# One head tile of lag, fewer DVE operations in attention, and edge columns and projection tiles placed elsewhere in the FFN

## The reference, cut to what matters

```python
xn = _layernorm(x, axis=-1)
x = x + attn(xn, ...) + ffn(xn, ...)

# attn, per head, Dh = 64
q = (x @ wq_w.T + wq_b); k = (x @ wk_w.T + wk_b); v = (x @ wv_w.T + wv_b)
attn = softmax(where(x[:, :, 0] != 0, q k^T / sqrt(Dh), -inf))
out = (attn @ v) @ wo_w.T + wo_b

# ffn
h = bit_linear(x, w1)                  # 1024 -> 4096, int8-like activations, ternary weights
h = depthwise_conv1d(h, conv_w, conv_b)   # width 3, over the tokens
h = silu(h)
return bit_linear(h, w2)               # 4096 -> 1024
```

## Time and profile before

| | |
|---|---|
| median of 3 runs | 1260.81 us (1182.61 to 1311.77) |
| the profiled execution | 1182.18 us, its slowest core (core 1) has a span of 1180.6 us |
| spans of the 8 cores | 1174.3 to 1180.6 us, granted PE clock 0.991 to 0.993 |
| PE busy | 1091.4 us (92% of the span) |
| DVE busy | 890.5 us (75%) |
| ACT busy | 815.8 us (69%) |
| POOL busy | 242.8 us (21%) |
| head | about 0 to 91 us |
| rest of attention | about 91 to 645 us |
| FFN block 0 | about 646 to 756 us |
| FFN blocks 1 to 3 and the tail | about 756 to 1181 us |

### The profile page before, as it was taken

How to read it: one execution, slowest core, us unless ns; L and a number is a source line. 1 busy time by engine, 2 the same in 40 slices (tenths; PEclk the granted TensorE clock), 3 DMA queues, 4 the chain that set the end, 5 groups by cost and what they waited for, 6 DMA issues and landing times.

```text
span 1180.6 us, 28483 instructions; the slowest of 8 cores (1174.3 to 1180.6 us)
## 1 busy us (share of the span) xinstructions
PE 1091.4 (92%) x9138; PEld 593.5 (50%) x9138; DVE 890.5 (75%) x1487; ACT 815.8 (69%) x1110; POOL 242.8 (21%) x263
## 2 busy tenths in 40 slices
PE   2679999999999999999988999989999999999998
PEld 2355655655565665655555444444444444444443
DVE  5437888988887888888851788877777777878866
ACT  3578888888888899899998545456666666556300
POOL 4220000000000000000012123233333333332684
PEclk9799999999999999999999999999999999999999
DMA  8535557555463767757673344574354545453452
GB/s 220 184 53 140 168 163 197 161 151 172 165 194 89 183 152 180 189 162 203 186 170 88 117 148 154 172 233 128 114 161 134 173 136 170 136 157 88 136 185 89
DMA packets 84061, 183.06 MB, mean 155 GB/s; under 512 B 24816, under 2 KB 28944, under 8 KB 83920
## 3 DMA queue, kind: packets, MB, share of 16 engines
q1 hardware_dynamic: 79248, 172.52, 48.3%
q0 software_dynamic: 4240, 8.69, 5.0%
q10 hardware_dynamic: 432, 0.04, 0.0%
HBM read 164.44 MB, written 25.17 MB: 161 GB/s over the span
## 4 chain that ended last, share of the span: by engine, by line
PE 67%; ACT 15%; issue 7%; DVE 7%; POOL 1%; DMA 1%; ACTq 0%; DVEq 0%; POOLq 0%; SPq 0%
PE psC L914 16%; PE psA L932 15%; ACT probs L405 14%; PE psS L500 11%; PE psV L517 5%; PE psQ L449 5%; PE psA L900 4%; PE psQ L465 3%; PE psQ L458 3%; PE psC L932 2%; DVE wsum L644 1%; DMA xhead<-x 1%; DVE u_sb L1067 1%; DMA strm<-x 1%; DVE xarea L1135 1%
## 5 line engine op out<-in xcount | busy, mean ns | idle before, releaser
L405 ACT ACTIVATE probs<-psS 128x1024 bf16<-128x1024 f32 x512 | 506.6, 1023 | 69.1 <-PE psS L500 52.7
L500 PE MATMUL psS<-qz,kroll 128*128 128x512 bf16 x1024 | 304.3, 378 | 18.7 <-ACT probs L405 14.0
L914 PE MATMUL psC<-xqT,w1q_sb 128*128 128x512 bf16 x1024 | 242.4, 381 | 0.0
L517 PEld LDWEIGHTS psV<-v_sb,probs 128*128 128x128 bf16 x4096 | 183.8, 97 | 77.9 <-issue 5.0
L932 PE MATMUL psA<-w2q_sb,hq 128*128 128x512 fp8e4 x896 | 212.6, 379 | 6.4 <-DVE hq L1118 6.2
L825 POOL TENSOR_TENSOR h_act<-h_act,shb_sb 128x512 f32<-128x512 f32 x128 | 165.4, 1296 | 229.0 <-DVE hq L1118 198.1
L517 PE MATMUL psV<-v_sb,probs 128*128 128x65 bf16 x4096 | 200.4, 194 | 1.7 <-DVE cn L633 0.6
L914 PEld LDWEIGHTS psC<-xqT,w1q_sb 128*128 128x128 fp8e4 x1024 | 99.1, 98 | 115.9 <-issue 1.9
L932 PEld LDWEIGHTS psA<-w2q_sb,hq 128*128 128x128 bf16 x896 | 87.0, 98 | 113.7 <-issue 10.8
L1067 DVE SCALAR_TENSOR_TENSOR u_sb<-psC,cws,u_sb 128x511 f32<-128x511 f32 x128 | 95.7, 748 | 62.0 <-ACT u_sb L850 61.9
L850 ACT ACTIVATE u_sb<-psC,cws 128x510 f32<-128x510 f32 (+2 forms) x128 | 87.5, 684 | 53.5 <-PE psX L924 52.3
(11 more groups left out here) (109 smaller groups left out, 1057.8 us busy)
## 6 DMA issues: line engine op xcount, KB each, us to landing
strm<-w_t SPq DMA_DIRECT2D x128, 512.0 KB, 4.7
w2q_sb<-w2q_stage SPq DMA_DIRECT2D x112, 256.0 KB, 2.6
w1q_sb<-w1q_stage SPq DMA_DIRECT2D x64, 256.0 KB, 3.1
xhead<-x SPq DMA_DIRECT2D x16, 512.0 KB, 7.1
strm<-x SPq DMA_DIRECT2D x16, 512.0 KB, 4.4
xarea<-x SPq DMA_DIRECT2D x16, 512.0 KB, 5.8
res_stage<-xarea SPq DMA_DIRECT2D x16, 512.0 KB, 3.1
xarea<-res_stage SPq DMA_DIRECT2D x16, 512.0 KB, 5.8
```

What stands on the lines that cost most here:

```text
L405: s.activation(out=probs[:, (i % NP) * 1024:(i % NP + 1) * 1024], in_=psS[:, b * 1024:(b + 1) * 1024], func=AF.Exp, scale=0.125, bias=-B0) ...
L500: mm = t.matmul(psS[:, b * 1024 + hh * 512:b * 1024 + (hh + 1) * 512], kTv[:, hp % 2, kc * 128:(kc + 1) * 128], qz[:, (it % 4) * 1024 + hh ...
L517: mm = t.matmul(psV[:, hh * 512 + qt * 65:hh * 512 + (qt + 1) * 65], probs[:, o:o + 128], v_v[:, kc, 2 * hp + hh, :], start=(kc == 0 and q ...
L914: mm = t.matmul(mbank(g), w1q_sb[:, o + cc * 256:o + cc * 256 + 128], xqTv[:, cc, tb * 512:tb * 512 + 512], start=(cc == 0), stop=(cc == N ...
```

## The change

It has two parts that touch different stages.

In attention:
- The scores, `exps` and `pv` of the head come one tile later (HS = 10), the first "q" job comes after tile 5 instead of 4, and DVE's evacuations stand two tiles further behind its `stats` (i - 7 instead of i - 5).
- The two operations that fill qz become one `scalar_tensor_tensor` over 128x1024 that adds the bias and multiplies by a mask `hmask` of ones and zeros. POOL writes that mask (four small memsets) instead of clearing qz.
- The column of V that holds the key mask is written for all 16 heads with the first "v" job of a tile, and no more with the others (48 small operations fewer).
- The two reciprocals after each block become one (32 fewer); of the four small operations of an "x" task two are left.
- The planner's costs are set lower to match (`part_us`, `evac_us`, `norm_us`).

In the FFN:
- In block 0 ACT's centre tap leaves out the last column and a second activation of one column, which adds the edge term as its bias, writes it; ACT waits for f_e before it. DVE's L1079 and its semaphore f_o3 fall away.
- Projection tiles 12 to 15 come ahead of slices 1 to 4 of block 1 instead of 0 to 3, on the PE and on DVE.

```diff
-    HS = NT - 5
+    HS = NT - 6
...
-        if i == 4:
+        if i == 5:
             head_after[i].append(("q", 0, 0))
...
-    part_us = {"w": [1.2], "x": [0.9, 1.2, 0.9, 1.8], "m": [0.3], "gap": [5.0],
+    part_us = {"w": [1.2], "x": [0.9, 1.2, 0.5, 1.8], "m": [0.3], "gap": [5.0],
                "z": [0.8, 0.8, 0.9]}
-    evac_us = {"k": 0.75, "q": 1.55, "v": 0.6, "t": 0.75, "x": 0.65, "m": 1.0}
-    norm_us = 1.5
+    evac_us = {"k": 0.75, "q": 1.2, "v": 0.5, "t": 0.75, "x": 0.65, "m": 1.0}
+    norm_us = 1.3
...
-        g.memset(qz[:], 0.0).then_inc(sem("qz0"), 1)
+        for h in range(2):
+            for m in range(2):
+                g.memset(hmask[64 * m:64 * m + 64, h:h + 1],
+                         1.0 if h == m else 0.0).then_inc(sem("hmask"), 1)
+        g.wait_ge(sem("hmask"), 4)
...
-            if i >= 6:
-                exps(i - 6)
+            if i >= 7:
+                exps(i - 7)
...
             elif g == HS:
                 t.wait_ge(sem("ln_e"), 2 * NT)
+                t.wait_ge(sem("p_e"), HS)
...
-            if i >= 7:
-                pv(i - 7)
+            if i >= 8:
+                pv(i - 8)
...
-            if i >= 5:
-                scores(i - 5)
+            if i >= 6:
+                scores(i - 6)
...
-                v.tensor_scalar(qz[0:64, o:o + 512], ps[0:64, :], bqc[0:64, hp:hp + 1], None,
-                                OP.add)
-                v.tensor_scalar(qz[64:128, o + 512:o + 1024], ps[64:128, :],
-                                bqc[64:128, hp:hp + 1], None, OP.add).then_inc(sem("pq_ev"), 1)
+                v.scalar_tensor_tensor(
+                    qz[:, o:o + 1024].rearrange("p (h t) -> p h t", h=2),
+                    ps.unsqueeze(1).to_broadcast([128, 2, 512]), bqc[:, hp:hp + 1],
+                    hmask[:].unsqueeze(2).to_broadcast([128, 2, 512]),
+                    OP.add, OP.mult).then_inc(sem("pq_ev"), 1)
...
-        for i in range(NT + 6):
+        for i in range(NT + 8):
             if i < NT:
                 stats(i)
-            if i == 5:
+            if i == 7:
                 v.wait_ge(sem("cstq"), 16 * 2)
-            if 5 <= i:
-                for job in head_after[i - 5]:
+            if 7 <= i:
+                for job in head_after[i - 7]:
                     evac(job)
...
-            s.activation(out=u_sb[:, o + lo:o + hi], in_=ps[:, lo:hi],
-                         func=AF.Identity, scale=c1, bias=0.0).then_inc(sem("f_c1"), 1)
+            mid = s.activation(out=u_sb[:, o + lo:o + hi], in_=ps[:, lo:hi],
+                               func=AF.Identity, scale=c1, bias=0.0)
+            if tb == 0:
+                s.wait_ge(sem("f_e"), jc + 1)
+                e = jc * 6 + 1
+                s.activation(out=u_sb[:, o + 511:o + 512], in_=ps[:, 511:512], func=AF.Identity,
+                             scale=c1, bias=edge[:, e:e + 1]).then_inc(sem("f_c1"), 1)
+            else:
+                mid.then_inc(sem("f_c1"), 1)
...
-                if tb == 1 and NPT + jc < NT:
-                    proj(NPT + jc)
+                if tb == 1 and 1 <= jc <= NT - NPT:
+                    proj(NPT + jc - 1)
...
-                tap3.then_inc(sem("f_o3"), 1)
-                v.wait_ge(sem("f_o3"), g + 1)
-                v.wait_ge(sem("f_e"), jc + 1)
-                v.tensor_tensor(ua[:, 511:512], ua[:, 511:512],
-                                edge[:, jc * 6 + 1:jc * 6 + 2], OP.add).then_inc(sem("f_cv"), 1)
...
+        def edges(jc):
+            v.wait_ge(sem("f_m1"), jc + 1)
+            v.tensor_tensor(edge[:, jc * 6:jc * 6 + 6], psX[:, jc * 6:jc * 6 + 6],
+                            cwe[:, jc * 6:jc * 6 + 6], OP.mult).then_inc(sem("f_e"), 1)
...
             for jc in (m1_after[ti - 1] if ti >= 1 else range(2)):
+                edges(jc)
                 conv(0, jc)
```

52 lines of the change are left out of this document (22 added, 30 removed).

## The result

The changed kernel takes 1162.01 us in the median of four runs. Its ratio to the kernel before, taken over comparable runs, is 0.9828, with a 95% interval of 0.9814 to 0.9842: 1.7% faster, some 20 us. (Slow runs are left out of every ratio: 1306.88 us of after, in which the four cores of one die had a granted clock of 0.833 to 0.839 and the others 0.995 to 0.997, and 1260.81 and 1311.77 us of before, which account for its high median.) The profiled execution took 1159.86 us, where the forecast was 1159 and the one of before took 1182.18. By the ratio the forecast is 2 to 3 us too low. Direction and size are near it, but as a sum of terms that missed on both sides: over the cores they add up to 21 us, where 23 were forecast. Times "over the cores" are means over the eight cores of the profiled execution.

The account below looks back on a forecast made before the run. It took a ring of PE, DVE, POOL and ACT to bound the head, mostly the PE the rest: 1182.2 - 14.1 (head) - 3.3 (rest of attention) - 2.0 (block 0) - 3.6 (step to block 1) = 1159.2, given as 1159; range 1151 to 1169.

Parts of the forecast that it names:

- Steps 1 to 4: Head: the predicted chain through first exponential at 42.9, norm(8) at 43.8 and head's end at 76.1, 15.1 us earlier.
- The -14.1: Head: the forecast's term for its total change in us, including the cost of one step fewer done there.
- step 5: Head: one step fewer is done by its end (HS = 10), costing 0.98 to 1.14 us, taken as 1.0.
- A: Rival in the head: it gains less, with a term of -7.8 us; chance 0.17.
- step 4: Head: norm(8) to the first exponential behind it falls from 38.6 to 32.3 us, including 3.3 from shorter waits.
- of 6.0 us and some smaller ones I take 3.3: Rest of attention: of the PE's waits for DVE's evacuations, lighter DVE work saves 3.3 us; bounds 0 and 7.
- Rival C: Attention and step to block 1: DVE's relief counts in full (-7), no late w2q (-5.3), total 1154; chance 0.20.
- rival D: Attention: the qz operation's double PSUM read through a broadcast makes DVE the bound, slower than before; chance 0.02.
- The 0.9 taken off for POOL: Block 0: gain cut by 0.9 of 2.9 us because `amax` may now wait for POOL, leaving -2.0.
- B: Rival in block 0: the round trip between DVE and ACT bounds it, +3 to +5 us; chance 0.13.
- delay x tiles 14 and 15 by some 3 us on SP and POOL, which costs DVE about 1 us where it waits anyway: Step to block 1: moved evacuations make these x tiles late, but the roughly 1 us falls in DVE's existing waiting.
- the 3.6 us over the cores: Step to block 1: second product begins at 784.7 instead of 788.33, a gain of 3.6 us; bounds -5.3 and 0.

## Why the prediction was right or wrong

**The sum.** That 1159 lies so near to 1159.86 is in part luck. The head gave 1.7 us less than forecast and the step to block 1 2.5 less, the rest of attention 1.5 and block 0 0.9 more, and 1159.86 is the lowest of the four runs of the changed kernel. Two steps of the prediction failed: what the PE's waits for DVE are worth in the rest of attention, with no term for the planner's new costs, and the wait of DVE at the step to block 1 that was held to cost nothing.

**The head: right in mechanism and places, a little large.** Steps 1 to 4 forecast the first exponential at 42.9 (43.27), norm(8) at 43.8 (44.19), waits of 1.05 around the "k" jobs (1.04 twice), the end at 76.1 (76.29), and the run with the order alone shows that this is the cause. The -14.1 was too large for two reasons. The profiled core of before ends its head at 91.2, 1.0 us later than the mean over the cores, and the slowest core of the whole execution need not be the one with the slowest head. And the exponential done later (step 5) cost 1.4 us, the difference of 13.8 at the head's end and 12.4 at the 37th exponential, not 1.0. The rival with a head of -7.8 (A, chance 0.17) is out: the end of the head came 13.8 us earlier over the cores.

The 3.3 us in step 4 are two waits, 2.98 and 2.46, less twice 1.05. That they were long because of the slow "k" was my estimate. The traces show the clock beside it: on the profiled core of before the first three "k" jobs of the head take 3.62, 3.60 and 3.04 us at granted clocks of 0.50 (34.80 to 38.42), 0.50 (55.77 to 59.30) and 0.61 (74.00 to 77.00), and the fourth 1.89 at 1.00 (87.83 to 89.70). On that of the changed kernel only the first is at 0.50, the next three take 1.67 to 1.89 at 1.00, and both waits are 1.04. What sets the granted clock, no run shows.

**The rest of attention: sign right, the term mis-sized and its cause incomplete.** The step that failed is "of 6.0 us and some smaller ones I take 3.3". The waits that name DVE were only a part; the same jobs' weight loads stood 20.6 us in front of psQ, under "issue". The relief by itself gives 5.0 where 3.3 was put. The forecast took the planner's new costs as following the operations and gave them no term: they cost 4.8 us, half of the 9.6 that relief and new order give together. The gain of the new order behind the head had no term either (3.5 alone). So the measured 4.8 is 9.6 less 4.8, and that it lies near 3.3 is no sign that the term was understood. Rival C had "all waits of the PE for it" at 7, where those that name DVE alone came to 10.8, and with the loads the waits fell by 17.7 for the 9.6 us.

**The qz operation**: 1.28 us against 1.25, 32 times, so rival D is out. The line against it, that every PSUM source takes 1.5 ns per element or less, did not fit, where 256 elements take 0.48 us (1.9 ns); it was right for operations of 512 (0.75 us, 1.5 ns) and 1024 (1.28 us).

**Block 0: right, on the safe side.** 2.9 against 2.0. By hand the PE waited 3.6 us for edges, it waits 2.4. The 0.9 taken off for POOL is borne out: on the profiled core `amax` took 1.52 to 2.17 us in five slices, each time ending 1.1 us behind POOL's addition, where on that of before it had 1.22 throughout, and taking the additions out gives 1.1. Without POOL the block is thus 4.0 us shorter than before, where the count by hand had 2.9: that part was too small, and POOL's was right. The rival in which the round trip between DVE and ACT bounds the block, at +3 to +5 us (B, chance 0.13), fell: the round trip is there as forecast, 0.6 us in 31 slices, but the PE waits only 2.4 us for edges, so it has the longer way.

**The step to block 1: wrong.** The step that failed is "delay x tiles 14 and 15 by some 3 us on SP and POOL, which costs DVE about 1 us where it waits anyway". DVE does not wait anyway there: between the last fold and the scales its work is on the path, and on each of the eight cores the addition for tile 14 meets one of its operations. The additions for tiles 14 and 15 moved from well ahead of the fold (they ended at 773.52 on the profiled core, the fold began at 775.85) onto `amax`, fold or evacuation, and took 2.31 us or more ahead of the evacuation, 1.95 on the fold or 1.0 on `amax`. Of the 3.6 us over the cores 1.1 was left. The sign "no wait at `chain_rows`" failed with it (1.55 us on the profiled core), that of 1 to 2 us for w2q held (1.98). The arrangement that I had in mind exists: with POOL out of the way the step is 29.3 us on every core, 2.7 less than before, and the remaining 0.9 to my 3.6 is partly the first rounded pair, for which the PE waits 1.56 to 1.76 us once w2q is early. The forecast counted on POOL's addition stretching an operation of DVE in block 0 alone (the 0.9 us taken off); the fold has two SBUF inputs like `amax`, and on cores 3 and 7 it takes 2.64 us instead of 0.69 beside the addition. The 16 matmuls behind the rows took 5.04 us before at a granted clock of 0.71 (783.45 to 788.33); in the changed kernel the clock there is 1.00 (760.30 to 765.40), and the 15 that were recorded take 3.40.

## What to carry to other kernels

After moving work later on one engine, follow the whole ring of its buffer (evacuation, store, load, the helper engine's operation) to where it now lands in time, and look what stands there on the engine whose operations get longer beside the helper's, as DVE's fold did here (2.64 us instead of 0.69 beside POOL's addition): 2.4 us of POOL off the path before became 2 us on it. Price a scheduler's new costs as an edit of their own, with the old costs as the first experiment; in these runs the costs nearer to the durations made the slower plan. And when you size what an engine's relief is worth, add the waits of the weight loads that stand under "issue" to those that name the engine; in these kernels half of what the sum fell by came off the time.

## What the runs showed of the hardware

POOL's addition and DVE's fold, which has two SBUF inputs, were measured in both orders, and the one that began later took longer. On the profiled core of the changed kernel the fold starts 0.17 us ahead and takes its 0.69, and two additions need 5.04 us instead of 4.7; on core 3 the addition starts 0.4 us ahead and the fold takes 2.64.

Not expected: DVE's rounding of a pair of slices, with one SBUF input (f32 to bf16, 512 columns), is stretched beside POOL's product on `h_act` too. On every core of both kernels 25 of the 128 roundings take 1.02 to 1.52 us, each ending 0.28 us behind a product of POOL that ran ahead of it, and the median is 0.54. Where the rounding starts 0.22 us ahead of a product, 11 times on each core, it takes 0.53 to 0.55, and the product 1.43 instead of 1.27. The first rounding of the kernel is one of the 25, as it was before the change (1.40 us at 785.87), so it is no part of what the change costs. A product starts 0.15 us ahead of it:

```profile
762.70 1.40 DVE L1118 TENSOR_SCALAR hq<-h_act,meff,meffneg 128x512 bf16<-128x512 f32 x1 [0.78 <-POOL h_act L831]
```

Why either operation gets longer beside POOL's, no run here shows.

One and the same program settles differently by core at the step: in the changed kernel, from block 0's end to `chain_max` it took 17.4 us on four cores and 18.4 to 19.3 on the others, according to which of DVE's operations met the addition, and with the POOL addition held 17.4 on all eight.
